# Mask loads of a two-layer graph kernel: a quadrant takes 512 columns of a whole turn in runs of 2 KB instead of 256 columns of a half turn in runs of 1 KB

## What is computed

```
h = relu(layernorm(x))
Wh = h @ W;  e = leaky_relu(Wh @ a1 + (Wh @ a2).T)
x = x + relu(softmax(where(adj > 0, e, -9e15)) @ Wh)        # attention
h = relu(layernorm(x))
node = h @ W1;  hw = einsum('nc,kcf->nkf', h, W2)
msg = einsum('nk,nkf->nf', node, hw)
out = x + relu(adj @ msg + node @ b)                         # messages
```

## Time and profile before

| | |
|---|---|
| median of 3 runs | 1779.82 us (1768.06 to 1789.03) |
| profiled execution | 1774.92 us, its span 1773.3 us |
| PE, DVE, ACT, POOL busy | 96%, 74%, 61%, 36% |
| setup, block 0, blocks 1 to 7, last stage | about 0 to 67, to 203, to 1254, to 1773 us |
| DMA traffic | 452.23 MB, mean 255 GB/s |

### The profile page before, as it was taken

The page is one execution under the profiler, slowest core; times in us unless marked ns, Lnnn a source line. Parts: engine busy times, 40 slices in busy tenths (PEclk is TensorE's granted clock), DMA queues, the critical chain, the costliest instruction groups (busy, mean ns, idle before and its releaser), DMA issues.

```text
span 1773.3 us, 36102 instructions
## 1 busy us (share of the span) xinstructions
PE 1709.6 (96%) x11311; PEld 1471.3 (83%) x11311; DVE 1316.8 (74%) x1775; ACT 1089.1 (61%) x1889; POOL 640.0 (36%) x522
## 2 busy tenths in 40 slices
PE   7999799999999999999999999999999999999998
PEld 4889688888888888888888888888777788888886
DVE  7778688899898898988888798888665543433534
ACT  4644476766666766667566667664556555555554
POOL 0000056455554655655545555655553300000000
PEclk9999899999999999999999999999999999999999
DMA  9999999999999999999999999996624444453430
GB/s 234 283 291 332 336 350 289 280 329 309 281 328 307 299 280 297 336 283 280 281 278 289 320 291 297 317 308 254 255 102 152 149 167 190 154 200 143 166 142 24
DMA packets 316753, 452.23 MB, mean 255 GB/s; under 512 B 21072, under 2 KB 291616, under 8 KB 298912
## 3 DMA queue, kind: packets, MB, share of 16 engines
q1 hardware_dynamic: 297664, 356.58, 73.1%
q10 hardware_dynamic: 12208, 75.62, 10.6%
q0 software_dynamic: 6832, 19.41, 3.4%
HBM read 364.46 MB, written 87.07 MB: 255 GB/s over the span
## 4 chain that ended last, share of the span: by engine, by line
PE 45%; SPq 15%; DMA 10%; DVE 10%; issue 9%; POOL 7%; ACT 2%; ACTq 0%; POOLq 0%; DVEq 0%
SPq L289 14%; PE ot_ps L800 14%; PE ot_ps L857 13%; PE mt_ps L857 13%; DMA keep_d<-keep 9%; DVE p_sb L989 6%; PE hw_ps L769 5%; POOL prod L399 5%; DVE mt L913 2%; DMA adj_sb<-in_adj_dram 1%; ACT prod L582 1%; POOL msg L402 1%; SPq L303 1%; DVE keep L970 1%; POOL msg L414 1%
## 5 line engine op out<-in xcount | busy, mean ns | idle before, releaser
L800 PEld LDWEIGHTS ot_ps<-wh_mask,p_sb 128*128 128x128 f32 x8192 | 947.2, 193 | 100.1 <-issue 86.2
L800 PE MATMUL ot_ps<-wh_mask,p_sb 128*128 (+1 forms) x8192 | 960.3, 277 | 35.2 <-DVE p_sb L989 21.8
L989 DVE SCALAR_TENSOR_TENSOR p_sb<-zb,qcol,mt 128x1024 f32<-128x1024 uint8 (+1 forms) x512 | 750.9, 1484 | 24.0 <-PE ot_ps L800 10.5
L399 POOL TENSOR_TENSOR prod<-prod 128x1024 f32<-128x1024 f32 (+2 forms) x192 | 383.9, 2000 | 499.4 <-ACT prod L582 441.1
L516 ACT ACTIVATE wh_mask<-adj_sb 128x2048 uint8<-128x2048 f32 x256 | 487.7, 1940 | 88.0 <-DMA adj_sb<-in_adj_dram 86.3
L1037 DVE CAST mask<-adj_sb 128x1024 fp32r<-128x1024 uint8 x272 | 204.0, 757 | 244.8 <-PE mt_ps L857 243.1
L609 ACT ACTIVATE mask<-adj_sb 128x1024 fp32r<-128x1024 uint8 x240 | 255.3, 1065 | 173.5 <-PE ot_ps L857 173.3
L582 ACT ACTIVATE prod<-hw_ps,node 128x128 f32<-128x128 f32 x1024 | 278.8, 384 | 116.0 <-PE hw_ps L769 115.0
L857 PE MATMUL mt_ps<-mask,msgs 128*128 128x512 f32 x1024 | 282.6, 398 | 2.1 <-DVE mask L1037 1.1
L857 PE MATMUL ot_ps<-mask,msgs 128*128 128x512 f32 x1024 | 274.8, 390 | 1.0 <-DVE mask L1037 0.5
L769 PE MATMUL hw_ps<-wcat,hT 128*128 128x512 f32 x512 | 242.4, 596 | 0.0
(11 more groups left out here) (108 smaller groups left out, 550.6 us busy)
## 6 DMA issues: line engine op xcount, KB each, us to landing
adj_sb<-in_adj_dram SPq DMA_DIRECT2D x1024, 256.0 KB, 7.6
maskT_d<-mt ACTq DMA_DIRECT2D x64, 1024.0 KB, 8.3
adj_sb<-maskT_d SPq DMA_DIRECT2D x32, 2048.0 KB, 7.8
keep_d<-keep POOLq DMA_DIRECT2D x64, 128.0 KB, 6.4
p_sb<-keep_d SPq DMA_DIRECT2D x4, 2048.0 KB, 12.1
msg_d<-msg POOLq DMA_DIRECT2D x56, 128.0 KB, 6.6
msgs<-msg_d SPq DMA_DIRECT2D x7, 1024.0 KB, 8.9
wh_mask<-in_x_dram SPq DMA_DIRECT2D x8, 512.0 KB, 9.5
```

What stands on the lines that cost most here:

```text
L399: pool.tensor_tensor(prod[:, 0:n, :], prod[:, 0:n, :], prod[:, n:2 * n, :], ALU.add)\
L800: ins = pe.matmul(ot_ps[h][:, (t - t0) * ROW:(t - t0 + 1) * ROW], p_sb[:, r, t * P:(t + 1) * P], rows, start=begin and t == t0, stop=end a ...
L989: dve.scalar_tensor_tensor(p_sb[:, r, :], zbf[:, bass.ds((ib % 2) * BLK, BLK)], qcol[:, bass.ds(tile + b_, 1)], mtb[:, p, k // 2, :, 2 * ( ...
```

## The change

Two half turns of before share what they load. A slot `c` of `adj_sb` now holds rows of one of four groups of 256 destination rows, and in it each partition quadrant has 512 neighbouring columns of the whole turn, in runs of 2 KB, where it had 256 columns of a half turn in runs of 1 KB. A slot is as large as before (2 MB) and is loaded by 4 transfers of 512 KB in place of 8 of 256 KB; a turn has 16 instead of 32. Both have 256 runs each. So that the two half turns find their sources, the rows are renumbered: a partition has 16 rows of `adj` in a row (it had 8), of which h = 0 belongs to the even and h = 1 to the odd block; rows of `x` that a partition reads are still 8 neighbouring ones of 4 KB, with as many of the other block between them and the next partition's. `m8` is one buffer for a whole turn in place of two for half turns. The squares of the second half turn are turned two by two in steps 0 and 1 of the first half turn, those of the next turn's first half two by two in steps 2 and 3 of the second half turn. The casts, as many and as large as before, are all put between step 1 of the first and step 1 of the second half turn. In the setup six casts stand ahead of the exponentials (five before), one between the exponentials and the copies of `zb`, one after them; the fourth square waits for the last of them, and the third for the sixth.

```
-    COLS = BLK // A
-    adj_v = adj.rearrange("(i c r t) n -> i c r t n", c=A, r=SQ, t=T)
-    x_v = x.rearrange("(i p t) f -> i p t f", p=P, t=T)
+    COLS = 2 * BLK // A
+    adj_v = adj.rearrange("(j c r h t) n -> j h c r t n", c=A, r=SQ, h=2, t=T)
+    x_v = x.rearrange("(j p h t) f -> j h p t f", p=P, h=2, t=T)
...
-        m8_squares = wh_mask[:, NT * (D + 2):].rearrange("p (h c t s y) -> p h c t y s", h=2, c=A, t=T, s=SQ)
+        m8_squares = wh_mask[:, NT * (D + 2):].rearrange("p (c t s w) -> p c t w s", c=A, t=T, s=SQ)
...
-            def load_adj(ib, jg, p, h):
-                load_quadrants(sp, ib, jg, p, h, (0, 2, 1, 3))
+            def load_adj(ib, jg, c):
+                for a in (0, 2, 1, 3):
+                    sp.dma_start(adj_sb[a * SQ:(a + 1) * SQ, c, :].rearrange("r (t n) -> r t n", n=COLS),
+                                 adj_v[bass.ds(ib // 2, 1), bass.ds(ib % 2, 1), c, :, :,
+                                       bass.ds(2 * BLK * jg + a * COLS, COLS)]
+                                 .rearrange("j h r t n -> (j h r) t n")).then_inc(adj_in[c], 16)
...
-                if i in (3, 5):
-                    load_adj(0, 0, 0, (i - 3) // 2)
+                if i in (4, 5, 7):
+                    load_adj(0, 0, {4: 0, 5: 1, 7: 2}[i])
...
+            load_adj(0, 0, 3)
...
-                for p in range(2):
-                    for h in range(2):
-                        q = 2 * p + h
-                        if not (isinstance(i, int) and i == 0 and p == 0):
-                            sp.wait_ge(adj_cast[q], i)
-                            load_adj(ib, jg, p, h)
+                for c in range(A):
+                    if not (isinstance(i, int) and i == 0):
+                        sp.wait_ge(adj_cast[c], i)
+                        load_adj(ib, jg, c)
...
-                if 2 <= i < 7:
-                    cast((i - 2) // 2, i % 2, 1, 0)
+                if i >= 2:
+                    cast((i - 2) // 2, i % 2, 0)
...
+            cast(3, 0, 0)
             for h in range(2):
                 act.wait_ge(z0_done, h + 1)
...
-                        ahead = None if last else lambda: cast(2 * p, 1, i + 2, A * n + A)
+                        ahead = None if last or p == 1 else lambda: cast(1, 0, i + 1)
...
-                        if k == 1 and not last:
-                            cast(2 * p, 0, i + 2, A * n + A)
-                        if k == 2 and not last:
-                            cast(2 * p + 1, 0, i + 2, A * n + A)
+                        if not last:
+                            for c, part in {(0, 1): ((0, 0), (0, 1)), (0, 3): ((1, 1),),
+                                            (1, 0): ((2, 0), (2, 1)), (1, 1): ((3, 0), (3, 1))}.get((p, k), ()):
+                                cast(c, part, i + 1)
...
-            for c in range(A):
-                dve.wait_ge(adj_cast[c // 2], 1)
+            for c in range(A - 1):
+                dve.wait_ge(adj_cast[c], 1)
                 turn_squares(0, c)
...
             scale_rows(0)
+            dve.wait_ge(adj_cast[A - 1], 1)
+            turn_squares(0, A - 1)
...
-                            turn_squares(1 - p, k)
+                        if p == 0 and k < 2:
+                            if k == 0 and not (isinstance(i, int) and i == 0):
+                                dve.wait_ge(mt_stored[1], 16 * i)
+                            for c in (2 * k, 2 * k + 1):
+                                turn_squares(1, c)
+                        if p == 1 and k >= 2 and not last:
+                            if k == 2:
+                                dve.wait_ge(mt_stored[0], 16 * i + 16)
+                            for c in (2 * k - 4, 2 * k - 3):
+                                dve.sem_inc(past_dve, 1)
+                                dve.wait_ge(adj_cast[c], i + 2)
+                                turn_squares(0, c)
```

More of the change, by code:

```diff
@@ L510, in take_wh, with cast @@
                                    ot_ps[g][:, 0:(t1 - t0) * (D + 2)], ACT.Copy).then_inc(wh_copied, 1)
-            def cast(q, part, count, squared_before):
-                act.wait_ge(adj_in[q], 16 * 2 * A * count)
-                act.wait_ge(squared, squared_before)
-                ins = act.activation(m8[:, q // 2, 2 * (q % 2) + part, :],
-                                     adj_sb[:, q, part * T * COLS:(part + 1) * T * COLS], ACT.Copy, scale=EDGE)
+            def cast(c, part, i):
+                act.wait_ge(adj_in[c], 16 * A * (i + 1))
+                if not (isinstance(i, int) and i == 0):
+                    act.wait_ge(squared, A * (2 * i - 1) + c + 1)
+                ins = act.activation(m8[:, c, part * BLK * 2:(part + 1) * BLK * 2],
+                                     adj_sb[:, c, part * BLK * 2:(part + 1) * BLK * 2], ACT.Copy, scale=EDGE)
                 if part == 1:
-                    ins.then_inc(adj_cast[q], 1)
+                    ins.then_inc(adj_cast[c], 1)
             deviation(0)
@@ L546, in _ @@
                 act.activation(zbf[:, h * HB:(h + 1) * HB], hw_ps[h][:, :], ACT.Copy).then_inc(z0_copied, 1)
-            cast(2, 1, 1, 0)
+            cast(3, 1, 0)
             act.activation(std[:, :], eps[:, :], ACT.Sqrt)
@@ L633, in turn @@
                             ahead()
-                        if isinstance(i, int) and i == 0 and p == 0 and k == 0:
-                            for part in range(2):
-                                cast(3, part, 1, 0)
-                        elif k == 0:
-                            if not (last and p == 1):
-                                cast(3 if p == 0 else 1, 1, i + 1 + p, A * n)
-                        if k == 1 and not last:
-                            cast(2 * p, 0, i + 2, A * n + A)
-                        if k == 2 and not last:
-                            cast(2 * p + 1, 0, i + 2, A * n + A)
+                        if not last:
+                            for c, part in {(0, 1): ((0, 0), (0, 1)), (0, 3): ((1, 1),),
+                                            (1, 0): ((2, 0), (2, 1)), (1, 1): ((3, 0), (3, 1))}.get((p, k), ()):
+                                cast(c, part, i + 1)
             attention_loop(act, turn)
```

27 lines of the change are left out of this document (7 added, 20 removed).

## The result

The changed kernel takes 1940.36 us (median of 4 runs, 1923.76 to 1951.19); before, on the same chip, 1773.94 us (1767.46 to 1789.03). The ratio is 1.0917, with a 95% interval from 1.0806 to 1.1028. The forecast was 1763 us, its range ended at 1791: it had sign and size wrong. The profiled execution took 1923.76 us, its span is 1922.2.

What follows compares the result with a forecast made beforehand. It took late mask loads to bound block 0, and a chain of PE, ACT, POOL and DVE without slack the later blocks. 1774.9 - 17.6 (block 0) - 8 (late loads) + 13.7 (turns) = 1763 us, range 1742 to 1791.

Steps and rivals of the forecast that it cites:

- Squares: Attention turns: wider read step taken as 0, ends 0 and 0.3 us more for each of two squares.
- 21 of the 28 turns: Finishing turns charged +0.65 us each for paired squares; the first of each block left out, its first tiles being weighed ahead.
- Loads at 0.85: Mask loads: with 2 KB runs a load takes 0.85 of its time, 7.4 us for 8.7; ends 1.0 and 0.73.
- The line through 1 KB and 8 KB: Queue q1 packet times fitted as 18.6 ns plus 40.8 ns for each 1000 bytes: 102 ns for 2 KB.
- rows 7 and 8: Profile rows of queue q1: block 0, 57.9 ns for 964 bytes; last stage, 354 ns for 8.2 KB.
- the runs don't matter: Rival on the loads: bytes or memory bound them, rate stays 242 GB/s, late loads stay; 1791 us, chance 0.22.
- -17.6: Block 0: earlier loads remove PE's gap, so it ends at 185.7 in place of 203.34 us.
- The 0.96: Mask loads by the Trainium skill's fixed packet cost: 0.96 of a load's time, moving the sum by +18 us.
- Setup: Before block 0: +5.3 us for waits on casts and squares, -2.6 us for earlier `x`; PE starts at 69.7.
- Late loads, -8: From block 1 on: the late-load part of 12 us goes, -8 us, bounds 0 and -12.
- Casts, +0.2: Second half turns: casts ahead of ACT's relu use up its slack, +0.2 us a turn, bounds 0 and 0.6.
- Bunches, +13.7: Squares two by two delay the step 2 weighing in first half turns; with the casts term +0.65 us a turn, +13.7 us.

Runs made afterwards that it cites:

- g5: g1 with the squares two by two, as in the changed kernel: 1827.71 us, ratio 1.014 to before.
- g7: The changed kernel with each slot loaded in two rounds over the quadrants, 256 KB a transfer: 1934.74 us, ratio 1.0858 to before.
- e1: The changed kernel with each square reading 8-byte steps from one half of its slot, mask columns those of other sources: 1872.86 us, ratio 1.0438 to before.
- e2: The changed kernel with casts that pack each half turn's columns, so squares read 8-byte steps with every source in its place: 1879.19 us, ratio 1.0527 to before.
- f1: Before with loads in runs of 2 KB, transfers still 256 KB, mask of other rows or columns: 1792.04 us, ratio 1.0015 to before.
- f2: Before with partitions 512 KB apart in `adj` (256 KB in before), runs still 1 KB, mask rows others: 1787.98 us, ratio 0.9968 to before.
- f5: Before with both 2 KB runs and partitions 512 KB apart in `adj`, mask mixed up: 1784.01 us, ratio 0.9959 to before.
- e3: e2 with one square in each step, as in before: 1877.95 us, ratio 1.0531 to before.
- g1: e3 with each slot loaded in two rounds over the quadrants, 256 KB a transfer, still 2 KB runs: 1815.54 us, ratio 1.0177 to before.
- g3: Before with the quadrants loaded in the order 0, 1, 2, 3 in place of 0, 2, 1, 3: 1819.86 us, ratio 1.0195 to before.

## Why the prediction was wrong

**Squares, the step that failed.** "The wider steps that a square reads with (16 bytes for 8) have no row; before reads with a step too, at 0.70; ends 0 and 0.3 us more for each of the two, I take 0." The term measured 0.40 us, above its upper end. Worse, it was weighed for two squares of a turn, those that lie ahead of a weighing PE waits for; the other six were taken as covered by DVE's idle time. That cover is small: in a whole turn of before DVE idles (900 - 790.6) / 900 x 37.5 = 4.6 us, and all eight squares grew at once, by 3.2 us in one stretch. From g5 to g7 96 of 105 us reached PE. The price decides 109 to 128 us with loads of 256 KB (g5 to g7), and with the changed kernel's own loads 61 to 85, by medians or ratios (changed to e1 or e2). Eight squares at the forecast's own end of 0.3, in 28 turns, would have been 67 us: the upper bound was there, and was multiplied by two where it should have been by eight.

**Two terms put at nothing.** The forecast counted 21 of the 28 turns, since the first tiles of a block are weighed ahead. But there the four squares stand ahead of step 2, and PE waits 5.1 to 5.3 us at six of the seven starts where before has at most 0.7, some 28 us in all. And PE's speed was taken as fixed, 115.0 us for a block's passes; with the new waits its clock falls again and again, and it was busy for 38.5 us more.

**Loads at 0.85, wrong.** The line through 1 KB and 8 KB gave 102 ns for a run of 2 KB; f1 has 123, the changed kernel 110, and a load of the changed kernel took 0.98 of its time in block 0. f1, f2 and f5 show no gain in the time. The rival "the runs don't matter" was right on this term: block 0 took 136.6 us from PE's start, before 137.3, and the forecast's -17.6 is +8.7. The 0.96 that the forecast also worked out, and turned down for rows 7 and 8, came nearer than the line did. What the forecast didn't ask is what the size of a transfer does: it counted runs and issues, saw that 8 of 256 KB become 4 of 512 KB, and put no price on it. That price is 62 us (e3 to g1), hidden in the changed kernel behind DVE (g7).

**Setup, mis-sized.** Forecast +5.3 - 2.6; measured 76.36 - 66.96 = +9.4. The two loads of 1.3 us that the seventh part of `x` was to gain became 3.5 us of delay: it was issued 2.5 us sooner (23.47 for 25.94), but q1 moved only 9.5 MB in the first 45 us for 10.4. From the maxima to the first weighing it is 11.1 us for 7.0, +4.1 where +2.7 was forecast, with one slow square in it.

**Late loads, -8.** Not seen. ACT waits less for them (50.2 us, 86.3 in before), only because the turn is longer; with fast squares and loads of 512 KB it waits 145.7 to 197.5 us (e1, e2, e3).

**Casts, +0.2, not contradicted.** ACT's deviation does come behind three casts, and DVE's `rstd` waits for it up to 2.0 us (59.1 us in 33 waits), a wait that the forecast hadn't named, as it looked at the relu. PE has work until then and waits for neither: from step 2 of a first half turn to step 2 of the second it is 18.1 to 19.1 us.

**Bunches, +13.7.** Open: g5 against g1 gives +12 us by the medians and nothing by the ratios. PE's waits for `p_sb` are 58.1 us in g5 and 41.0 in g1, which fits a small price.

**What stays open.** g1, with fast squares, spread squares and loads of 256 KB, is still 1.8% slower than before. By its blocks (first end 225.6 instead of 204.3, then 152.4 us for 149.9) 21 us lie in setup and block 0, where f1, f2 and f5 show 12 to 20 without being slower, and 17 us in the rest. Casts in bunches, fewer free slots and slots that need all their rows before the first cast are candidates, and none was tried alone. Open is also why e3 moves less than g3 in the steady blocks. No version tried beats before.

## What to carry to other kernels

When an edit changes the step of an operand, its price has no row in the trace of before: time that one operation with both steps before the forecast, or let its upper end run over all instances, not only over those next to a wait. Cover is a sum, and all that grows in a stretch draws on the same idle time. When an engine that was always busy begins to wait, look at its granted clock too: the loss can be larger than the waits. When transfers are merged, ask which partitions each one fills and for how long, not only how many runs and bytes it has.
